# A one-core hybrid block kernel: three small moves in the order of the work at the start and the end of its mixer loop

## The chip, the cores and the metric

The kernel runs on one core of a Trainium2 chip. The metric is the device time of one execution in microseconds; of several executions the median is taken. TensorE (PE) multiplies matrices, VectorE (DVE), ScalarE (ACT) and GpSimd (POOL) do element-wise work, and SyncE (SP) issues the DMAs. Each engine runs its own instruction list in order, and the lists are tied together by semaphores: an instruction that waits holds up everything behind it on its engine.

## The reference

The reference computes a block with four parts, each added to a residual stream x of 2 x 512 tokens by 512 channels:

```python
x = x + masked_linear(layernorm(x))
x = x + ffn(layernorm(x))        # 4-bit weights, dequantized by group; silu(gate) * up, then down
x = x + mixer(layernorm(x))      # Mamba-2 style state space mixer
x = x + ffn(layernorm(x))        # the same weights
```

The mixer is most of the time. It projects the normalised tokens to a gate z, to x, B and C and to dt, runs a causal convolution of four taps with a silu over x, B and C, and works in chunks of 128 tokens:

```python
Y_diag = einsum('bclsh,bcshp->bclhp', (C @ B.T) * exp(segment_sum(A_dt)), x_dt)
Y_off  = einsum('bclhn,bchpn->bclhp', C, states) * state_decay
y = Y_diag + Y_off + D * x
y = y * rsqrt(mean(y ** 2) + eps) * norm_w
y = y * silu(gate)
out = y @ out_proj_w.T
```

There are 128 heads of 64 channels (8192 channels), 8 groups of B and C, and two batches of 512 tokens.

## The kernel before

**Precision.** Every large product is made of float32r operands split in two: a high part (a copy by ScalarE into float32r) and a low part (the value minus its high part). A product of two such operands is three matmuls per 128 rows of the contraction, `PASSES`: high by high, high by low, low by high. A projection of 512 channels has 4 x 3 = 12 matmuls of 128x512.

**Steps.** The mixer walks over 128 pairs of heads, k = 0 to 127 (K = 128), 64 to a batch, plus five steps to drain (`STEPS` = K + 1 + HALF = 133). A pair is 128 channels. In step k TensorE (`tensor`, in the class `Mixer`) does, in this order:

- `project(("x", k + 1))`: the projection of the next pair's x (L1016)
- `outputs(k - 1)`: y of the pair before (L1085, L1091)
- `turn_x(k)`: x turned to tokens by channels (L1056)
- `project(("z", k + 1))`: the gate of the next pair (L1016), and in some steps the projection of a group's B or C. `bc_units(k)` gives B of group 1 in step 3 and C of group 1 in step 4, and the later groups likewise, eight steps apart
- `project_out(i, t)`, one tile of the output projection (L1104)
- `states(k)`: the chunk states (L1069)

**Output projection.** Four pairs make a half group (`HALF` = 4), so there are 32 of them, i = 0 to 31. One half group's contribution to the four token tiles t = 0 to 3 of its batch is made one tile per step, four steps after its last pair. A tile is 4 pairs x 3 passes = 12 matmuls into one of three ring banks of PSUM; then VectorE adds it to the residual (`accumulate`, L1549). `project_out` waits until `yg_lo`, the count of low parts of y, and `wo_lo`, the count of low parts of output weights, have reached all four pairs. The last half group (i = 31, pairs 124 to 127) has its tiles in steps 129 to 132, when no pair is left to work on.

**VectorE** (`vector`) in step k: `y_low(k - 2)` (the low part of the gated y of two pairs before, L1538, which waits for `yg_hi`, ScalarE's high part), the accumulation of an output tile, `decay_c(k)` (L1511), `conv(("x", k + 1))` (three instructions, L1458, which wait for `tap_done`), `scale_x(k)` (x_dec and x_dt, L1479 and L1484) and `mask_em(k)` (L1519), `gate(k - 1)` (y and the gated y, which is written over sz, L1528 and L1532), `carry(k)` (the state carried over chunks, L1493 and L1499), and in steps 3 and 4 the convolution of B or C.

**ScalarE** (`scalar`) in step k: high parts of weights (`w_high`, L1243, and `wo_high`, L1311), `tap(("x", k + 1))` (the first tap of the convolution, out of the ring bank, L1255), `clamp(k + 1)` (eight small instructions, L1285), in an odd step `exponent(k + 1)` (L1295), `activate_x(k + 1)` (silu of x, L1260), `activate_z(k + 1)` (silu of the gate into `sz`, L1265), `y_high(k - 1)` (L1305) and `square(k - 1)` (L1299), which wait for the gated y, then in steps 3 and 4 the tap of B or C, and in an even step `exponent(k + 1)`. Exp and Silu need different function tables; the loads of these show as ACT_TABLE_LOAD.

**The buffer behind one wait.** `sz` has three slots. `activate_z` writes slot k % 3, so it has to wait until the low part of the pair three before has been read from it:

```python
def activate_z(k):
    act.wait_ge(prj_mm, UNIT["z", k] + 1)
    need(act, yg_lo, k - 2)
```

In step 2 it makes z of pair 3, which needs `yg_lo` at 1: `y_low(0)`, which VectorE does at the head of the same step.

**GpSimd** makes the low parts of the weights (L1688, L1693) and the running sum of y squared (L1705). **SyncE** loads the weights; a load waits until the slot's low part has been made, and of those slots there are two.

**After the last pair**, TensorE in step 128 turns two tiles of the second FFN's normalised input (L128), and in step 129 does the first tile of the last half group, `square_sums(1)` (eight products with a column of ones, L1118), and turns two more tiles. VectorE's `factor_mean(1)` (L1581) and `factor(1)` (L1587) and between them ScalarE's `factor_root(1)` (L1385, a square root with its own table) make the norm's factor out of these sums; `end_tile` (L1599) then finishes each token tile, and the second FFN (`ffn`, L410 and L422) begins. Its first products need all eight normalised tiles in high and low parts (`norm_low`, L140).

## Time and profile before

| | |
|---|---|
| median of 3 runs | 2114.71 us (2114.70 to 2115.32) |
| the profiled execution's own time | 2115.85 us |
| its span, from first to last instruction | 2114.1 us |
| TensorE busy | 2067.3 us, 98% of the span |
| VectorE, ScalarE, GpSimd busy | 78%, 67%, 42% |
| mean granted TensorE clock | 0.998 of 2.4 GHz |

The share of the clock is 1.00 for 2.4 GHz and 0.50 for 1.2 GHz. In a timeline row stand the start in us, the time in us, the engine, the line, the operation, what is written and read with its shape, the number of instructions merged in the row, and in brackets the idle time of the engine before it and who ended it. A row's time reaches to the end of its last instruction, while the next may have started. In the trace step 2 begins on TensorE at 333.80 us, step 5 at 372.32 us, and step 129 at 1862.62 us.

### The profile page before, as it was taken

How to read it: one execution, taken by the hardware profiler on the slowest of the kernel's cores; microseconds unless marked ns; L12 is line 12 of the kernel's file. 1: busy time of each engine (PE TensorE's matmuls, PEld its weight loads, DVE VectorE, ACT ScalarE, POOL GpSimd, SP SyncE). 2: the span in 40 equal slices, each digit the busy share in tenths (PEclk: the TensorE clock that was granted, in tenths of full speed). 3: DMA queues.
4: the chain of work that ended last, by engine and by line, in shares of the span. 5: the costliest groups of instructions: out<-in, count | busy, mean ns of one | idle time of the engine just before them, and what ended most of it. 6: DMA issues, size and time to landing. Idle time of an engine off the chain costs nothing.

```text
span 2114.1 us, 35693 instructions
## 1 busy us (share of the span) xinstructions
PE 2067.3 (98%) x12366; PEld 1703.4 (81%) x12366; DVE 1656.5 (78%) x2676; ACT 1424.1 (67%) x2690; POOL 887.6 (42%) x616
## 2 busy tenths in 40 slices
PE   7999998999999999999999999999999999989999
PEld 6788876788888888888888888888888888878887
DVE  7655557888888888888888888888888888876554
ACT  4322268878787878778787877877877878742221
POOL 1221214445454545454454544454545555422121
PEclk9999999999999999999999999999999999999999
DMA  5543225445444444444444444445444444455341
GB/s 204 176 139 136 78 85 184 151 140 158 147 138 154 139 154 148 150 160 133 142 156 150 144 155 134 150 154 162 139 155 140 154 149 145 148 172 172 131 147 40
DMA packets 160095, 307.06 MB, mean 145 GB/s; under 512 B 14528, under 2 KB 47552, under 8 KB 159680
## 3 DMA queue, kind: packets, MB, share of 16 engines
q1 hardware_dynamic: 159936, 305.00, 44.4%
q8 instruction: 92, 1.51, 0.3%
q14 instruction: 67, 0.55, 0.1%
HBM read 299.70 MB, written 5.24 MB: 144 GB/s over the span
## 4 chain that ended last, share of the span: by engine, by line
PE 78%; DVE 10%; issue 5%; ACT 4%; POOL 1%; DMA 1%; DVEq 0%; ACTq 0%; SPq 0%; POOLq 0%
PE ring L1016 30%; PE ring L1104 14%; PE bank L410 6%; PE bank_e L410 6%; PE yt L1085 5%; PE st L1069 4%; PE bank_e L422 3%; PE yt L1091 3%; PE bank L422 3%; PE xt L1056 3%; DVE xc L1458 1%; DVE ce L1511 1%; DVE em L1519 1%; DVE ygs L1538 1%; DVE bc L1458 1%
## 5 line engine op out<-in xcount | busy, mean ns | idle before, releaser
L1016 PE MATMUL ring<-m_lnt,w_sb 128*128 128x512 f32 x3456 | 858.9, 398 | 5.5 <-ACT sz L1265 2.5
L1016 PEld LDWEIGHTS ring<-m_lnt,w_sb 128*128 128x128 f32 x3456 | 630.1, 188 | 134.0 <-issue 3.1
L1688 POOL TENSOR_TENSOR w_sb<-w_raw,w_sb 128x512 fp32r<-128x512 f32 x288 | 428.4, 1490 | 162.3 <-ACT w_sb L1243 162.0
L1705 POOL TENSOR_TENSOR ysq<-ysq,y 128x512 f32<-128x512 f32 x126 | 169.8, 1348 | 637.2 <-ACT y L1299 637.2
L1104 PE MATMUL ring<-wo,ygs 128*128 128x512 f32 x1536 | 372.2, 392 | 5.6 <-DVE ygs L1538 3.3
L1104 PEld LDWEIGHTS ring<-wo,ygs 128*128 128x128 f32 x1536 | 289.2, 189 | 68.0 <-issue 7.8
L1458 DVE SCALAR_TENSOR_TENSOR xc<-ring,cw,xc 128x511 f32<-128x511 f32 (+2 forms) x384 | 286.8, 747 | 52.3 <-ACT xc L1255 43.2
L1285 ACT ACTIVATE cum_b<-cum_b,cum_q 128x128 f32<-128x128 f32 x1024 | 312.5, 390 | 0.0
L1243 ACT ACTIVATE w_sb<-w_raw 128x512 fp32r<-128x512 f32 x288 | 178.2, 620 | 48.0 <-DMA w_raw<-w_in 47.8
L1693 POOL TENSOR_TENSOR wo<-wo_raw,wo 128x512 fp32r<-128x512 f32 x128 | 191.1, 1493 | 1.6 <-ACT wo L1311 1.6
L1085 PE MATMUL yt<-em,x_dt 128*64 128x128 f32 x2048 | 183.9, 279 | 3.6 <-DVE state L1499 3.5
L326 POOL TENSOR_TENSOR f_gu<-f_gu_f,f_gu 128x1024 fp32r<-128x1024 f32 x28 | 67.3, 2404 | 257.7 <-ACT f_gu L349 257.7
L1511 DVE TENSOR_TENSOR ce<-ce,bc 128x768 f32<-128x768 f32 x128 | 171.6, 1340 | 1.9 <-DMA ce<-e_t 1.8
L1295 ACT ACTIVATE arg<-cum_b 128x1024 f32<-128x1024 f32 x128 | 131.8, 1029 | 60.8 <-DVE em L1519 59.6
L1305 ACT ACTIVATE ygs<-sz 128x512 fp32r<-128x512 f32 x128 | 80.2, 626 | 128.5 <-DVE sz L1532 126.4
L1085 PEld LDWEIGHTS yt<-em,x_dt 128*64 128x64 f32 x2048 | 118.5, 136 | 49.0 <-issue 49.0
L1519 DVE TENSOR_TENSOR em<-arg,gt 128x1024 f32<-128x1024 f32 x128 | 155.6, 1215 | 0.0
L410 PE MATMUL bank_e<-f_lnt,f_gu 128*128 128x512 f32 x672 | 154.3, 390 | 0.7 <-DVE f_lnt L140 0.7
L410 PE MATMUL bank<-f_lnt,f_gu 128*128 128x512 f32 x672 | 154.2, 390 | 0.6 <-DVE f_lnt L140 0.6
L1091 PE MATMUL yt<-ce,state 128*64 128x128 f32 x1536 | 149.7, 273 | 0.0
L410 PEld LDWEIGHTS bank_e<-f_lnt,f_gu 128*128 128x128 f32 x672 | 125.9, 188 | 27.1 <-DVE f_lnt L140 1.1
L410 PEld LDWEIGHTS bank<-f_lnt,f_gu 128*128 128x128 f32 x672 | 125.9, 188 | 27.1 <-DVE f_lnt L140 1.1
(198 smaller groups left out, 2891.9 us busy)
## 6 DMA issues: line engine op xcount, KB each, us to landing
w_raw<-w_in SPq DMA_DIRECT2D x288, 256.0 KB, 3.4
cum_b<-c_t SPq DMA_DIRECT2D x128, 512.0 KB, 4.6
ce<-e_t SPq DMA_DIRECT2D x128, 384.0 KB, 4.5
wo_raw<-w_out SPq DMA_DIRECT2D x128, 256.0 KB, 3.0
f_gu_q<-gu_w SPq DMA_DIRECT2D x28, 512.0 KB, 3.5
f_gu_zr<-gu_z SPq DMA_DIRECT2D x28, 512.0 KB, 4.3
f_gu_sr<-gu_s SPq DMA_DIRECT2D x28, 512.0 KB, 5.3
f_dn_q<-dn_w SPq DMA_DIRECT2D x28, 256.0 KB, 3.4
```

Of the source, the lines that this page charges most:

```text
L410: mm = nc.tensor.matmul(dst[half][:], gu[:, j, b, c:c + P], lnt[:, a, k, half * TOK:(half + 1) * TOK], start=(i == 0), stop=(i == 3 * KT - 1))
L1016: mm = nc.tensor.matmul(dst[:], w_sb[:, u % WR, wp, k * P:(k + 1) * P], lnt[:, xp, k, b * S:(b + 1) * S], start=(i == 0), stop=(i == 3 * K ...
L1085: mm = nc.tensor.matmul(YT[h * HD:(h + 1) * HD, c * CS:(c + 1) * CS], x_dt[:, at:at + HD], em[:, h, c * CS:(c + 1) * CS], start=True, stop ...
L1091: mm = nc.tensor.matmul(YT[h * HD:(h + 1) * HD, c * CS:(c + 1) * CS], state[:, c - 1, h * HD:(h + 1) * HD], ce[:, k % 2, h, (c - 1) * CS:c ...
L1104: mm = nc.tensor.matmul(dst[:], ygs[:, j % OR, yp, t * P:(t + 1) * P], wo[:, j % WOR, wp], start=(m == 0), stop=(m == 3 * HALF - 1))
L1243: nc.scalar.activation(w_sb[:, u % WR, 0], w_raw[:, u % NR], ACT.Copy).then_inc(w_hi, 1)
L1285: last = nc.scalar.activation(cum_b[:, k % 2, h, at], cum_b[:, k % 2, h, at], ACT.Relu, scale=-1.0, bias=cum_q[:, k, c, h:h + 1])
L1458: nc.vector.scalar_tensor_tensor(out=dst[:, d:S], in0=src[:, 0:S - d], scalar=cw[:, tile, j:j + 1], in1=dst[:, d:S], op0=ALU.mult, op1=ALU ...
L1511: nc.vector.tensor_tensor(ce[:, k % 2], ce[:, k % 2], c_off.rearrange("p (o t) -> p o t", o=1) .to_broadcast([P, 2, OFFC * CS]), ALU.mult) ...
L1519: nc.vector.tensor_tensor(em[:], ARG[:], gt[:, k // QG % 2].rearrange("p (o t) -> p o t", o=1).to_broadcast([P, 2, S]), ALU.mult).then_inc ...
L1688: nc.gpsimd.tensor_tensor(w_sb[:, u % WR, 1], w_raw[:, u % NR], w_sb[:, u % WR, 0].bitcast(F32), ALU.subtract).then_inc(w_lo, 1)
L1693: nc.gpsimd.tensor_tensor(wo[:, j % WOR, 1], wo_raw[:, j % 2], wo[:, j % WOR, 0].bitcast(F32), ALU.subtract).then_inc(wo_lo, 1)
```

## The change

There are three parts.

1. `project_out` for the first tile of the last half group (i = 31, t = 0) waits at first for one pair less in both counts, and waits for the fourth pair ahead of matmul 9, the first of its own three.
2. On VectorE `y_low(k - 2)` moves, for k = 2, 3 and 4, from the head of the step to behind `carry(k)`. From step 5 on it stays at the head.
3. On ScalarE the tap of B of group 1 (step 3) moves from behind `square(2)` to ahead of `activate_x(4)`. The other taps of B and C stay.

```diff
--- before.py
+++ after.py
@@ -1097,10 +1097,14 @@
                 def project_out(i, t):
                     dst = ring_bank(("out", (i, t)))
                     ring_free(("out", (i, t)))
-                    pe.wait_ge(yg_lo, HALF * (i + 1))
-                    pe.wait_ge(wo_lo, HALF * (i + 1))
+                    early = 1 if (i, t) == (K // HALF - 1, 0) else 0
+                    pe.wait_ge(yg_lo, HALF * (i + 1) - early)
+                    pe.wait_ge(wo_lo, HALF * (i + 1) - early)
                     for m, (j, (yp, wp)) in enumerate((j, ab) for j in range(HALF * i, HALF * (i + 1))
                                                       for ab in PASSES):
+                        if early and m == 3 * (HALF - 1):
+                            pe.wait_ge(yg_lo, K)
+                            pe.wait_ge(wo_lo, K)
                         mm = nc.tensor.matmul(dst[:], ygs[:, j % OR, yp, t * P:(t + 1) * P], wo[:, j % WOR, wp],
                                               start=(m == 0), stop=(m == 3 * HALF - 1))
                     mm.then_inc(out_mm, 1)
@@ -1411,6 +1415,8 @@
                     if k + 1 < K:
                         if k % 2:
                             exponent(k + 1)
+                        if k == 3:
+                            tap(("b", 1))
                         activate_x(k + 1)
                         activate_z(k + 1)
                     if 1 <= k <= K:
@@ -1419,7 +1425,8 @@
                     for unit in ahead[2:]:
                         w_high(unit)
                     for unit in bc_units(k):
-                        tap(unit)
+                        if k != 3:
+                            tap(unit)
                     for g in silu_in(k):
                         activate_bc(g)
                     if k + 1 < K and k % 2 == 0:
@@ -1623,7 +1630,7 @@
                             norm_shift(dve, n, i)
                     if k == K + 2:
                         factor_mean(1)
-                    if 2 <= k <= K + 1:
+                    if HALF < k <= K + 1:
                         y_low(k - 2)
                     if k == K + 1:
                         scale_gu(0, 0)
@@ -1667,6 +1674,8 @@
                         carry(k)
                     if k == 0:
                         conv(("x", 2))
+                    if 2 <= k <= HALF:
+                        y_low(k - 2)
                     if k == K - 1:
                         sub_gu(0, 0)
                     for g in gram_in(k):
```

**TensorE, end of step 128 and step 129.** bank_e5 is a turned tile of the FFN's input, ring1 the bank of the output tile, ysq the sum of squares. Before:

```order
L128 MATMUL bank_e5<-ident,f2_xn 128x128 [waits n2_xn_done,xdt_done]
L128 MATMUL bank_e5<-ident,f2_xn 128x128 x3
L1104 MATMUL ring1<-wo,ygs 128x512 [waits wo_lo,yg_lo,acc_done]
L1104 MATMUL ring1<-wo,ygs 128x512 x11
L1118 MATMUL arg<-ones,ysq 128x1 [waits em_done,ysq_done]
L1118 MATMUL arg<-ones,ysq 128x1 x3
L128 MATMUL bank_e6<-ident,f2_xn 128x128 [waits n2_xn_done,st_done]
```

Of the change:

```order
L128 MATMUL bank_e5<-ident,f2_xn 128x128 [waits n2_xn_done,xdt_done]
L128 MATMUL bank_e5<-ident,f2_xn 128x128 x3
L1108 MATMUL ring1<-wo,ygs 128x512 [waits wo_lo,yg_lo,acc_done]
L1108 MATMUL ring1<-wo,ygs 128x512 x8
L1108 MATMUL ring1<-wo,ygs 128x512 [waits wo_lo,yg_lo]
L1108 MATMUL ring1<-wo,ygs 128x512 x2
L1122 MATMUL arg<-ones,ysq 128x1 [waits em_done,ysq_done]
L1122 MATMUL arg<-ones,ysq 128x1 x3
L128 MATMUL bank_e6<-ident,f2_xn 128x128 [waits n2_xn_done,st_done]
```

The wait for the fourth pair stood ahead of all twelve matmuls and now stands ahead of the last three.

**VectorE, from the carry of step 1 to that of step 2.** ygs<-sz,ygs is `y_low`, ce is `decay_c`, state is `carry`. Before:

```order
L1493 COPY state<-st 128x128
L1499 SCALAR_TENSOR_TENSOR state<-state,e_last,st 128x64 x4
L1538 TENSOR_TENSOR ygs<-sz,ygs 128x512
L1511 TENSOR_TENSOR ce<-ce,bc 128x768
L1458 SCALAR_TENSOR_TENSOR xc<-ring2,cw,xc 128x511
L1458 SCALAR_TENSOR_TENSOR xc<-ring2,cw,xc 128x510
L1458 SCALAR_TENSOR_TENSOR xc<-ring2,cw,xc 128x509
L1479 TENSOR_TENSOR x_dec<-xt,dec_q 128x384
L1484 TENSOR_TENSOR x_dt<-xt,dt_q 128x512
L1519 TENSOR_TENSOR em<-arg,gt 128x1024
L1528 SCALAR_TENSOR_TENSOR y<-xc,d_col,yt 128x512
```

Of the change:

```order
L1518 TENSOR_TENSOR ce<-ce,bc 128x768
L1465 SCALAR_TENSOR_TENSOR xc<-ring2,cw,xc 128x511
L1465 SCALAR_TENSOR_TENSOR xc<-ring2,cw,xc 128x510
L1465 SCALAR_TENSOR_TENSOR xc<-ring2,cw,xc 128x509
L1486 TENSOR_TENSOR x_dec<-xt,dec_q 128x384
L1491 TENSOR_TENSOR x_dt<-xt,dt_q 128x512
L1526 TENSOR_TENSOR em<-arg,gt 128x1024
L1535 SCALAR_TENSOR_TENSOR y<-xc,d_col,yt 128x512
L1539 SCALAR_TENSOR_TENSOR sz<-y,nw,sz 128x512
L1500 COPY state<-st 128x128
L1506 SCALAR_TENSOR_TENSOR state<-state,e_last,st 128x64 x4
L1545 TENSOR_TENSOR ygs<-sz,ygs 128x512
```

The low part of pair 0 stood ahead of ce, and now stands behind the carry of step 2; what was behind that carry, the low part of pair 1, has gone behind the next.

**ScalarE, step 3 from the exponent on.** bc is B's tap, sz<-ring2 `activate_z(4)`, ygs<-sz `y_high(2)`. Before:

```order
L1295 ACTIVATE arg<-cum_b 128x1024 [waits em_done,arg_clamped]
L1260 ACT_TABLE_LOAD
L1260 ACTIVATE xc<-xc 128x512 [waits conv_done]
L1265 ACTIVATE sz<-ring2 128x512 [waits yg_lo,prj_mm]
L1305 ACTIVATE ygs<-sz 128x512 [waits yg_done]
L1299 ACTIVATE y<-y 128x512 [waits yg_done]
L1243 ACTIVATE w_sb<-w_raw 128x512 [waits prj_mm,w_loaded1]
L1255 ACTIVATE bc<-ring0,cb,cw 128x512 [waits prj_mm]
L1243 ACTIVATE w_sb<-w_raw 128x512 [waits prj_mm,w_loaded0]
L1311 ACTIVATE wo<-wo_raw 128x512 [waits wo_loaded0]
L1255 ACTIVATE xc<-ring1,cb,cw 128x512 [waits y_done,prj_mm]
```

Of the change:

```order
L1299 ACTIVATE arg<-cum_b 128x1024 [waits em_done,arg_clamped]
L1259 ACTIVATE bc<-ring0,cb,cw 128x512 [waits prj_mm]
L1264 ACT_TABLE_LOAD
L1264 ACTIVATE xc<-xc 128x512 [waits conv_done]
L1269 ACTIVATE sz<-ring2 128x512 [waits yg_lo,prj_mm]
L1309 ACTIVATE ygs<-sz 128x512 [waits yg_done]
L1303 ACTIVATE y<-y 128x512 [waits yg_done]
L1247 ACTIVATE w_sb<-w_raw 128x512 [waits prj_mm,w_loaded1]
L1247 ACTIVATE w_sb<-w_raw 128x512 [waits prj_mm,w_loaded0]
L1315 ACTIVATE wo<-wo_raw 128x512 [waits wo_loaded0]
L1259 ACTIVATE xc<-ring1,cb,cw 128x512 [waits y_done,prj_mm]
```

B's tap has moved ahead of the table load and the two silus; no table load is added.

## Rows read from the trace of the kernel before

**Rows 1.** The page: the span, and each engine's busy time.

```profile
span 2114.1 us, 35693 instructions
...
PE 2067.3 (98%) x12366; PEld 1703.4 (81%) x12366; DVE 1656.5 (78%) x2676; ACT 1424.1 (67%) x2690; POOL 887.6 (42%) x616
```

**Rows 2.** Waits of TensorE (who, for whom: us, times, longest).

```profile
PE st L1069 <- DVE x_dec L1479: 7.8, 8, 2.5
```

**Rows 3.** Windows view, steps 6 to 126: busy times, granted clock, DMA.

```profile
385.00:1845.00 1460.00, 1454.50 (x9466) 1201.03 (x9466) 1253.50 (x2058) 1170.28 (x2273) 731.95 (x510) 1.00 0.46 148
```

**Rows 4.** Timeline of TensorE, steps 2 to 5 (start, us, what, idle before).

```profile
344.27 0.94 PE L1069 MATMUL st<-x_dec,b_tok 128*128 128x128 f32 x6 [2.25 <-DVE x_dec L1479]
...
356.50 0.83 PE L1069 MATMUL st<-x_dec,b_tok 128*128 128x128 f32 x6
...
371.63 0.94 PE L1069 MATMUL st<-x_dec,b_tok 128*128 128x128 f32 x6 [2.47 <-DVE x_dec L1479]
...
382.94 2.97 PE L1104 MATMUL ring<-wo,ygs 128*128 128x512 f32 x12 [1.64 <-POOL wo L1693]
```

**Rows 5.** Timeline of ScalarE, the same steps.

```profile
344.67 0.59 ACT L1265 ACTIVATE sz<-ring 128x512 f32<-128x512 f32 x1
347.42 0.63 ACT L1305 ACTIVATE ygs<-sz 128x512 fp32r<-128x512 f32 x1 [2.17 <-DVE sz L1532]
...
362.94 0.77 ACT L1255 ACTIVATE bc<-ring,cb,cw 128x512 f32<-128x512 f32 x1
...
364.64 0.77 ACT L1255 ACTIVATE xc<-ring,cb,cw 128x512 f32<-128x512 f32 x1
...
374.78 0.63 ACT L1305 ACTIVATE ygs<-sz 128x512 fp32r<-128x512 f32 x1 [2.52 <-DVE sz L1532]
...
379.39 0.62 ACT L1311 ACTIVATE wo<-wo_raw 128x512 fp32r<-128x512 f32 x1
```

**Rows 6.** Timeline of VectorE, the same steps.

```profile
348.52 0.68 DVE L1538 TENSOR_TENSOR ygs<-sz,ygs 128x512 fp32r<-128x512 f32 x1
...
353.20 2.32 DVE L1458 SCALAR_TENSOR_TENSOR xc<-ring,cw,xc 128x511 f32<-128x511 f32 x3 [2.05 <-ACT xc L1255]
...
363.74 2.32 DVE L1458 SCALAR_TENSOR_TENSOR bc<-ring,cw,bc 128x511 f32<-128x511 f32 x3 [3.36 <-ACT bc L1255]
...
368.81 2.30 DVE L1458 SCALAR_TENSOR_TENSOR xc<-ring,cw,xc 128x511 f32<-128x511 f32 x3
```

**Rows 7.** Timeline of TensorE, steps 129 on and the FFN's start.

```profile
1862.62 5.46 PE L1104 MATMUL ring<-wo,ygs 128*128 128x512 f32 x12 [3.32 <-DVE ygs L1538]
...
1869.89 8.44 PE L1104 MATMUL ring<-wo,ygs 128*128 128x512 f32 x36
...
1886.29 16.62 PE L410 MATMUL bank_e<-f_lnt,f_gu 128*128 128x512 f32 x72 [0.69 <-DVE f_lnt L140]
```

**Rows 8.** Windows view, TensorE's first product of step 129.

```profile
1862.00:1868.00 6.00, 5.38 (x14) 4.25 (x14) 4.54 (x5) 4.49 (x7) 3.36 (x2) 0.50 0.74 262
```

**Rows 9.** Timeline of VectorE, steps 129 to 132.

```profile
1861.83 0.69 DVE L1538 TENSOR_TENSOR ygs<-sz,ygs 128x512 fp32r<-128x512 f32 x1 [0.69 <-ACT ygs L1305]
...
1865.27 1.27 DVE L140 TENSOR_TENSOR f_lnt<-bank_e,f_lnt 128x512 fp32r<-128x512 f32 x2
1869.24 0.16 DVE L1581 TENSOR_SCALAR eps_row<-arg 128x4 f32<-128x4 f32 x1 [2.70 <-PE arg L1118]
...
1869.92 0.17 DVE L1587 RECIPROCAL eps_row<-eps_row 128x4 f32<-128x4 f32 x1
...
1878.36 0.69 DVE L1549 TENSOR_TENSOR xr<-xr,ring 128x512 f32<-128x512 f32 x1 [0.33 <-PE ring L1104]
```

**Rows 10.** Timeline of ScalarE, steps 129 and 130.

```profile
1867.27 1.28 ACT L1385 ACT_TABLE_LOAD   x1
1869.43 0.21 ACT L1385 ACTIVATE eps_row<-eps_row 128x4 f32<-128x4 f32 x1 [0.89 <-DVE eps_row L1581]
```

## Prediction

> **What bounds the kernel now.** I read the page first. TensorE is busy for 2067.3 of 2114.1 us [rows 1], so all its idle time is 46.8 us, and a change of order can only win from that. Next came the windows view. From step 6 to step 126 TensorE is busy for 1454.5 of 1460 us at the full clock [rows 3]. A delay or a gain that reaches TensorE before 385 us is therefore kept to the end of the loop, since there is next to no idle time to swallow it. The view of waits puts 7.8 us on `states` waiting for x_dec [rows 2], and the timeline shows where: 2.25 us in step 2 and 2.47 us in step 4, then 1.64 us ahead of the first output tile [rows 4]. Last, the one long wait behind the loop: 3.32 us for the low part of y of pair 127, in step 129 [rows 7]. The change touches these two places, and I cost each by walking through it. A measurement of this kernel can tell a difference of about 0.2%, 4.2 us, from none; both terms below are smaller.
>
> **Low parts behind the carry: a new wait on ScalarE.** The move takes no work away. In step 2 VectorE gets to its convolution of x(3) sooner, but that waits for ScalarE's tap anyway, so `states(2)` stays at 344.27. What the move adds is behind `activate_z(3)`. It needs the low part of pair 0, and began at 344.67 [rows 5]. The low part of pair 0 now stands where that of pair 1 stood, right behind the carry of step 2: 348.52 to 349.20 [rows 6]. So ScalarE waits until 349.2, spends 0.5 us on z, and comes to `y_high(1)` at 349.7 in place of 347.42 [rows 5]. Of the 4.5 us wait, 2.17 us was idle time of ScalarE before; **2.3 us** is new delay. Queued behind it are the high part of B's weights, the exponent of step 3 and the tap of x(4).
>
> **Step 3.** The convolution of x(4) began at 353.20 after 2.05 us idle for that tap [rows 6], so it goes to 355.5. TensorE's `states(3)` began at 356.50 with no wait [rows 4]. From the step 4 pair of rows, `states` can begin 2.82 us behind the start of the convolution (368.81 to 371.63) [rows 4, 6]; so it could have begun at 356.0, and now begins at 358.3, 1.8 us later. The carry of step 3 and the low part of pair 1 behind it end at about 363.3, just as ScalarE comes to `activate_z(4)`, so there the slot costs nothing more.
>
> **B's tap ahead of the silus.** The tap was at 362.94 and the convolution of B at 363.74, after 3.36 us idle of VectorE [rows 5, 6]. The tap costs 0.77 us wherever it stands. In its new place it starts about when the exponent ends, at 361.3 with the delay. VectorE is free at 363.3, so the convolution of B ends at 365.5 and the decayed C (up to 2.0 us) at 367.5. The tap of x(5) ends at 364.64 + 0.77 + 2.3 = 367.7 [rows 5], and this now rules: the convolution of x(5) begins at 367.7 in place of 368.81 [rows 6], 1.1 us sooner. Moving the tap by itself would bring it to the tap's old end, 365.4, **3.4 us** sooner; the low parts take 2.3 of it back. TensorE's wait of 2.47 us in step 4 goes, but what is late next is ScalarE.
>
> **Step 4 and the first output tile.** `y_high(3)` was released by the gated y at 374.78, after 2.52 us idle [rows 5]. VectorE is 1.1 us sooner, but `activate_z(5)` ahead of it again waits for a low part behind the carry, the same pattern as in step 2, worth +2.3. So `y_high(3)` is at 374.78 - 1.1 + 2.3 = 376.0, 1.2 us late. Behind it stand the tap of C, the exponent and the high part of the output weights of pair 3 (379.39) [rows 5], which GpSimd's low part and the first output tile wait for. That tile began at 382.94 and was waiting for exactly this [rows 4]. **The first part costs 1.2 us.** Its bounds: 0.9 if B's weights go through GpSimd faster; 1.5 if VectorE's decayed C is slowed more.
>
> **The last half group.** The first three pairs are ready: pair 126's low part lands as the turns of step 128 end, at about 1859.1. Nine matmuls at full clock are 9 x 8.44 / 36 = 2.1 us [rows 7] and fill the wait to 1861.2. The low part of pair 127 ends at 1862.5 [rows 9]; the last three end at 1863.3. Before, the twelve took 5.46 us [rows 7] with the clock at 0.50, 1.2 GHz [rows 8], after the 3.32 us in which TensorE did nothing, and ended at 1868.1. So the product ends **4.8 us sooner**, 2.1 by the early start, the rest by the clock, if that stays up. But who waits for it? The sums of squares follow, and VectorE's mean stood at 1869.24 after 2.70 us idle [rows 9]. It can now run when `norm_low` ends, at 1865.27 + 1.27 = 1866.5 [rows 9]. ScalarE's root is behind its table load, which ends at 1867.27 + 1.28 = 1868.6 [rows 10], 0.9 us before the old 1869.43. VectorE's reciprocal stood at 1869.92 [rows 9], behind the accumulation of the first tile, which can now run ahead of it: it goes to 1868.6 + 0.2 = 1868.8, 1.1 us sooner. The rest of the end is VectorE's own chain, whose one wait for TensorE, 0.33 us at 1878.36 [rows 9], goes too. TensorE has its 36 matmuls [rows 7] done by 1876 and waits no less for VectorE at 1886.29 [rows 7]. **The end gains 1.1 + 0.33 = 1.4 us** out of 4.8.
>
> **The sum.** 2115.85 (the profiled execution, 1.75 above its span) + 1.2 - 1.4 = 2115.65. That execution was 1.14 above the median of the runs, 2114.71, so the forecast is **2114.5**: no change that can be told.
>
> **Where a rule of the skill speaks.** In this trace the clock was at 1.2 GHz after TensorE had stood idle, and TensorE worked its way back up [rows 7, 8]. The Trainium skill, "TensorE: Matmul & The Clock Gate", section "What's actually happening", says the low clock is the default and that activity releases it. By that rule a wait cut into pieces need not be enough; this is the second case.
>
> **The cases.**
> - *Forecast, 0.65.* Both walks hold: +1.2 and -1.4, 2114.5.
> - *The clock falls in the new gaps, 0.14.* The product ends sooner, so TensorE now stands idle behind it: from 1863.3 until the turn, whose input ScalarE makes at 1866.5, but for eight short products. If it falls there, some eight of the next 36 matmuls run at 5.46 / 12 = 0.455 us in place of 0.234 [rows 7], 1.8 us. They would end at 1877.8, and of the end's 1.4 us only 0.3 stays. Time: 2114.71 + 1.2 - 0.3 = 2115.6. For it: much idle, little work there. Against: with 2.25 and 2.47 us idle at a time in steps 2 and 4 [rows 4] the products behind ran at full pace.
> - *The new wait on ScalarE costs nothing, 0.12.* If the idle time that I count as used up is there after all, only B's tap counts: y_high(3) comes 3.4 sooner less about 1.0 for ScalarE's own queue, -2.4, and with the end -3.8: 2110.9. It speaks against it that the slot's wait is in the code.
> - *Slower, 0.09.* The one mechanism is the sz slot of step 2, with B's tap not making up for it. If VectorE, not the tap, bounds step 4 (B's convolution begins no sooner than 365.5, because it still waits for the tap), the convolution of x(5) is 2.3 late in place of 1.1 early. Then step 4's pattern adds 2.3 on top: +4.6, which is slower by over 0.2% if the end gains under 0.4, as when the clock falls. With the end's 1.4 it is 2117.9, with 0.3 it is 2119.0. The point from which it decides is that start of B's convolution, 365.5 against my 363.3.
>
> **Numbers.** The forecast with the clock's case spans 2113 to 2116.5. The range reaches down to near the third case and up towards the fourth: 2112.0 to 2117.2. Faster by over 0.2% needs the third case and more than its 3.8 us: 0.04. Slower by over 0.2% needs the fourth with little gained at the end: 0.05. Within 0.2%: 0.91.
>
> **What would show it.** Step by step: `activate_z(3)` with 4.5 us idle of ScalarE ended by VectorE's ygs, and `y_high(1)` 2.3 us late; `states(3)` about 1.8 us late, with a wait; `states(4)` without its 2.47 us; the first output tile about 1.2 us late. At the end nine matmuls, a gap of some 1.4 us and three at 2.4 GHz; the FFN's product of 1886.29 sooner by 1.4 us, counted from the turns of step 128. I am wrong if ScalarE does not wait in step 2, if the output tile is early, or if the clock is at 0.50 anywhere behind 1863.

## The result, and the profile after

| | before | after |
|---|---|---|
| median of the runs, us | 2114.93 (2112.54 to 2117.79, 16 runs) | 2118.98 (2117.28 to 2120.84, 16 runs) |
| profiled execution, us | 2115.85 | 2119.61 |
| its span, us | 2114.1 | 2117.9 |

The ratio is 1.0017, with a 95% interval of 1.0011 to 1.0024. The change makes the kernel about 4 us slower. That is 0.17 to 0.19%, just inside the 0.2% that the prediction called telling, but the interval excludes one. The prediction was 2114.5 with a range up to 2117.2, and the result is outside it. Of all the executions behind this document one, of experiment e8, took 2578.33 us at a mean granted clock of 0.754; it is left out of that run's ratio, and without it the median of e8 would be 2112.23 in place of 2112.29.

The page of the changed kernel, span and busy times:

```profile
span 2117.9 us, 35694 instructions
...
PE 2070.2 (98%) x12366; PEld 1705.2 (81%) x12366; DVE 1655.0 (78%) x2676; ACT 1424.8 (67%) x2690; POOL 888.2 (42%) x616
```

With the same 12366 matmuls TensorE is *busy* for 2.9 us more than in [rows 1]. An order that only made TensorE wait longer would add idle time. More busy time for the same matmuls points to the clock, so that is the first thing to look for.

To place the 4 us I cut both traces at the same instructions. **S** runs from the start of `states(2)` to the start of `states(5)`. **E** runs from the start of `states(127)` to the start of the FFN's product of 72 matmuls at L410. What lies between is the loop.

| us | before | after | difference |
|---|---|---|---|
| S | 41.47 | 45.54 | +4.07 |
| from there to `states(127)` | 1466.19 | 1466.29 | +0.10 |
| E | 34.36 | 34.13 | -0.23 |

The three add up to +3.94; the spans differ by 3.8, since `states(2)` itself starts 0.17 sooner after the change. S is 385.74 - 344.27 before and 389.64 - 344.10 after.

TensorE in the changed kernel, steps 2 to 5 (start, us, what, idle before and who ended it):

```profile
344.10 0.94 PE L1069 MATMUL st<-x_dec,b_tok 128*128 128x128 f32 x6 [2.25 <-DVE x_dec L1486]
...
358.24 0.94 PE L1069 MATMUL st<-x_dec,b_tok 128*128 128x128 f32 x6 [1.73 <-DVE x_dec L1486]
...
371.48 0.83 PE L1069 MATMUL st<-x_dec,b_tok 128*128 128x128 f32 x6
...
377.41 3.01 PE L1016 MATMUL ring<-m_lnt,w_sb 128*128 128x512 f32 x12
384.38 5.46 PE L1108 MATMUL ring<-wo,ygs 128*128 128x512 f32 x12 [3.96 <-POOL wo L1702]
389.64 1.21 PE L1069 MATMUL st<-x_dec,b_tok 128*128 128x128 f32 x6
```

Measured from `states(2)`, `states(3)` is 1.91 us late against [rows 4] (14.14 against 12.23), `states(4)` is as early as before and without its wait of 2.47 us, and the first output tile is 1.61 late (40.28 against 38.67). So far this is close to the walk. The row of the tile is not: in front of it TensorE is idle for 3.96 us where it was idle for 1.64, and the twelve matmuls take 5.46 us where they took 2.97 [rows 4].

ScalarE of the changed kernel, the same steps:

```profile
349.13 0.60 ACT L1269 ACTIVATE sz<-ring 128x512 f32<-128x512 f32 x1 [4.52 <-DVE ygs L1545]
349.63 0.62 ACT L1309 ACTIVATE ygs<-sz 128x512 fp32r<-128x512 f32 x1
...
371.29 0.63 ACT L1247 ACTIVATE w_sb<-w_raw 128x512 fp32r<-128x512 f32 x1 [3.85 <-DMA w_raw<-w_in]
...
375.75 0.60 ACT L1269 ACTIVATE sz<-ring 128x512 f32<-128x512 f32 x1 [0.96 <-DVE ygs L1545]
376.25 0.62 ACT L1309 ACTIVATE ygs<-sz 128x512 fp32r<-128x512 f32 x1
...
380.86 0.61 ACT L1315 ACTIVATE wo<-wo_raw 128x512 fp32r<-128x512 f32 x1
```

VectorE of the changed kernel, step 3:

```profile
363.10 2.31 DVE L1465 SCALAR_TENSOR_TENSOR bc<-ring,cw,bc 128x511 f32<-128x511 f32 x3
...
367.47 2.32 DVE L1465 SCALAR_TENSOR_TENSOR xc<-ring,cw,xc 128x511 f32<-128x511 f32 x3
```

The wait for the slot of sz is there, 4.52 us, and makes `y_high(1)` 2.4 late against [rows 5], again measured from `states(2)`. The convolution of B goes without its wait of 3.36 us [rows 6], and that of x(5) begins 1.2 sooner. In step 4 the pattern returns (0.96 us for the low part of pair 2), and the high part of the output weights of pair 3, at 380.86 in place of 379.39 [rows 5], is 1.6 late. So it is this that the first output tile waits for, by way of GpSimd.

One row here is in no step of the prediction: at 371.29 ScalarE has waited 3.85 us for a load of weights. Before, it stood here:

```profile
367.74 0.63 ACT L1243 ACTIVATE w_sb<-w_raw 128x512 fp32r<-128x512 f32 x1 [2.33 <-DMA w_raw<-w_in]
```

Measured from `states(2)` it is 3.7 us later. A load waits until GpSimd has made the low part of its slot, and GpSimd waits for ScalarE, so a delay of ScalarE in steps 2 and 3 comes back to it by way of the weights. Behind this row ScalarE stood idle for 0.43 and 2.52 us before, and for 0.96 us now; 3.7 less 2.95 plus 0.96 is 1.7 us, close to the measured 1.6 of `y_high(3)`.

The clock of TensorE, changed kernel, windows view (window; its length; busy us of TensorE, weight loads, VectorE, ScalarE and GpSimd; granted clock; DMA share; GB/s): the gap ahead of the first output tile, the tile, and three stretches of the end:

```profile
380.30:384.40 4.10, 0.14 (x2) 0.05 (x1) 3.74 (x6) 4.10 (x12) 3.37 (x3) 0.90 0.67 150
384.40:389.60 5.20, 5.20 (x12) 4.09 (x13) 3.69 (x6) 4.45 (x9) 1.08 (x1) 0.50 0.73 227
1868.00:1872.00 4.00, 2.31 (x14) 2.25 (x14) 3.21 (x6) 3.20 (x4) 2.08 (x1) 0.55 1.01 360
1872.00:1875.00 3.00, 3.00 (x10) 2.42 (x10) 2.07 (x4) 1.73 (x4) 0.28 (x1) 0.50 1.02 276
1875.00:1878.00 3.00, 3.00 (x14) 2.52 (x13) 2.02 (x4) 0.00 (x0) 0.00 (x0) 0.96 1.03 272
```

All of the first output tile ran at 0.50, that is at 1.2 GHz; the clock fell in the gap ahead of it, whose mean is 0.90. At the end it fell again, about 1868: the prediction's own sign of being wrong, a clock of 0.50 behind 1863, is in the row from 1872.

TensorE of the changed kernel, steps 129 on:

```profile
1863.18 2.33 PE L1108 MATMUL ring<-wo,ygs 128*128 128x512 f32 x9
1866.57 0.97 PE L1108 MATMUL ring<-wo,ygs 128*128 128x512 f32 x3 [1.06 <-DVE ygs L1545]
1867.72 1.27 PE L1122 MATMUL arg<-ones,ysq 128*128 128x1 f32 x8 [0.19 <-POOL ysq L1714]
1870.69 1.94 PE L128 MATMUL bank_e<-ident,f_xn 128*128 128x128 f32 x8 [1.70 <-ACT f_xn L120]
1872.28 9.80 PE L1108 MATMUL ring<-wo,ygs 128*128 128x512 f32 x36
...
1890.06 16.62 PE L410 MATMUL bank_e<-f_lnt,f_gu 128*128 128x512 f32 x72 [0.67 <-DVE f_lnt L140]
```

VectorE of the changed kernel, steps 130 to 132:

```profile
1870.47 0.15 DVE L1588 TENSOR_SCALAR eps_row<-arg 128x4 f32<-128x4 f32 x1
...
1872.80 0.18 DVE L1594 RECIPROCAL eps_row<-eps_row 128x4 f32<-128x4 f32 x1 [1.59 <-ACT eps_row L1389]
...
1876.68 0.69 DVE L1556 TENSOR_TENSOR xr<-xr,ring 128x512 f32<-128x512 f32 x1 [0.94 <-PE ring L1108]
...
1882.12 0.69 DVE L1556 TENSOR_TENSOR xr<-xr,ring 128x512 f32<-128x512 f32 x1 [0.33 <-PE ring L1108]
```

The product is split as planned, nine and three, at full pace. Then TensorE waits for ScalarE's f_xn, and the 36 matmuls take 9.80 us in place of 8.44 [rows 7]. VectorE waits for them twice, once for 0.94 us where it had no wait. Counted from `states(127)`, 4.00 us later in this trace, the reciprocal of the norm's factor stands at 1868.80, exactly where the walk put it, 1.1 us sooner than before. The wait of 0.94 us takes nearly all of that back.

### The profile page after: what moved, and what is told of

It reads as the page before. It is cut to its first block, busy times and chain, and to the rows that moved or that the text cites. A ratio compares the mean times of both kernels' runs of the same rounds, so it can differ in the third digit from the quotient of the medians.

```text
span 2117.9 us, 35694 instructions
## 1 busy us (share of the span) xinstructions
PE 2070.2 (98%) x12366; PEld 1705.2 (81%) x12366; DVE 1655.0 (78%) x2676; ACT 1424.8 (67%) x2690; POOL 888.2 (42%) x616
## 4 chain that ended last, share of the span: by engine, by line
PE 80%; DVE 10%; issue 5%; ACT 4%; POOL 1%; DMA 0%; DVEq 0%; ACTq 0%; SPq 0%; POOLq 0%
PE ring L1016 30%; PE ring L1108 14%; PE bank L410 6%; PE bank_e L410 6%; PE yt L1085 5%; PE st L1069 4%; PE bank_e L422 3%; PE yt L1091 3%; PE xt L1056 3%; PE bank L422 3%; DVE xc L1465 1%; DVE em L1526 1%; DVE ce L1518 1%; DVE ygs L1545 1%; DVE bc L1465 1%
## 5 line engine op out<-in xcount | busy, mean ns | idle before, releaser
L410 PE MATMUL bank_e<-f_lnt,f_gu 128*128 128x512 f32 x672 | 154.4, 390 | 0.7 <-DVE f_lnt L140 0.7
L410 PE MATMUL bank<-f_lnt,f_gu 128*128 128x512 f32 x672 | 154.1, 390 | 0.6 <-DVE f_lnt L140 0.6
L410 PEld LDWEIGHTS bank_e<-f_lnt,f_gu 128*128 128x128 f32 x672 | 125.9, 188 | 27.2 <-DVE f_lnt L140 1.1
L410 PEld LDWEIGHTS bank<-f_lnt,f_gu 128*128 128x128 f32 x672 | 125.9, 188 | 27.1 <-DVE f_lnt L140 1.1
```

The lines of the kernel that those rows point to most:

```text
L410: mm = nc.tensor.matmul(dst[half][:], gu[:, j, b, c:c + P], lnt[:, a, k, half * TOK:(half + 1) * TOK], start=(i == 0), stop=(i == 3 * KT - 1))
```

## The experiments

The theory at this point: of the 4.07 us in S, about 1.6 is the order (the wait for the slot less what B's tap gives), carried through to the first output tile, and about 2.4 (5.46 - 2.97 = 2.49) is the clock. At the end the clock takes back what the early start gives. The rival: the order alone costs the whole, and the clock only shows where TensorE would wait anyhow, so that keeping it up changes nothing.

All twelve in one table. "Tile" is the idle time ahead of the first output tile and its length; "last" is the product of step 129 and the 36 matmuls behind. S, E and these lengths are of one profiled execution each. Each median stands beside runs of before on the same chip (medians 2114.77, 2115.26 and 2115.4 for the three groups that ran together, 32 to 35 runs each).

| run | median us | ratio, 95% | S | tile | E | last |
|---|---|---|---|---|---|---|
| before | - | - | 41.47 | 1.64 / 2.97 | 34.36 | 5.46, 8.44 |
| the change | 2118.98 | 1.0017, 1.0011 to 1.0024 | 45.54 | 3.96 / 5.46 | 34.13 | 2.33 + 0.97, 9.80 |
| e1 end alone | 2117.0 | 1.0003, 0.9994 to 1.0012 | 41.42 | 1.62 / 3.00 | 34.27 | 2.32 + 0.97, 9.94 |
| e2 first steps alone | 2118.72 | 1.0014, 1.0005 to 1.0023 | 45.48 | 3.97 / 5.46 | 33.15 | 4.57, 8.46 |
| e3 low parts alone | 2120.39 | 1.0026, 1.0016 to 1.0035 | 46.28 | 3.96 / 4.58 | 33.14 | 4.39, 8.44 |
| e4 tap alone | 2114.58 | 0.9997, 0.9988 to 1.0006 | 42.15 | 2.88 / 5.46 | 32.55 | 3.00, 8.42 |
| e5 change, gap filled | 2116.57 | 1.0010, 1.0001 to 1.0018 | 43.12 | 0.47 / 3.01 | 33.64 | 2.32 + 0.98, 9.47 |
| e6 change, fourth slot | 2114.93 | 0.9999, 0.9990 to 1.0008 | 39.82 | 2.88 / 3.01 | 34.59 | 2.33 + 0.96, 10.27 |
| e7 tap, gap filled | 2112.92 | 0.9992, 0.9983 to 1.0001 | 39.81 | 0.21 / 2.97 | 33.19 | 4.38, 8.47 |
| e8 tap, end split, both filled | 2112.29 | 0.9985, 0.9977 to 0.9994 | 39.75 | 0.23 / 2.99 | 32.57 | 2.32 + 0.96, 8.43 |
| e9 before, end filled | 2114.25 | 0.9996, 0.9987 to 1.0005 | 41.32 | 1.62 / 3.00 | 32.55 | 3.00, 8.43 |
| e10 change, first tile split | 2117.69 | 1.0009, 1.0000 to 1.0018 | 41.96 | 1.59 / 0.93 for the last three | 34.48 | 2.31 + 0.96, 10.14 |
| e11 tap, both split, end filled | 2112.35 | 0.9984, 0.9975 to 0.9993 | 38.68 | 0.90 / 0.94 for the last three | 32.55 | 2.31 + 0.96, 8.45 |
| e12 as e11, with the low parts and a fourth slot | 2112.0 | 0.9983, 0.9974 to 0.9992 | 38.58 | 0.88 / 0.93 for the last three | 32.54 | 2.31 + 0.96, 8.43 |

The loop between S and E took 1465.7 to 1467.7 in all of these, without a pattern that I could see. S and E leave that scatter out and so tell more than the medians, but each is one execution.

**The parts apart: e1 to e4.** e1 has only the split of the last product; e2 only the first steps:

```
-                    early = 1 if (i, t) == (K // HALF - 1, 0) else 0
+                    early = 0
```

e3 has, of the first steps, only the low parts behind the carry, and e4 only B's tap; both with `early = 0`. In e3 B's tap goes back:

```
-                        if k == 3:
-                            tap(("b", 1))
...
-                        if k != 3:
-                            tap(unit)
+                        tap(unit)
```

and in e4 the low parts:

```
-                    if HALF < k <= K + 1:
+                    if 2 <= k <= K + 1:
                         y_low(k - 2)
...
-                    if 2 <= k <= HALF:
-                        y_low(k - 2)
```

Expected of e1:

> Only the split wait of the last half group's first tile; both moves of the first steps undone. Theory (the clock falls once more behind the product, as in the trace of the change, 0.60 in 1868 to 1870 us): 0.2 to 0.3 us faster than before, the FFN's first long product sooner by the same, the 36 matmuls behind in 9.8 us. Rival (that fall came of where the first steps had left the rest of the program; alone the split keeps the clock up): 1.4 us faster, the 36 matmuls in 8.4 us.

Of e2:

> Both moves of the first steps, without the split wait. Theory (the sz slot costs 1.6 us up to the first output tile, and the 3.96 us that TensorE then stands idle bring it to 1.2 GHz for that tile, 5.46 us in place of 2.97): 4.1 us slower than before, first output tile at 5.4 to 5.5 us. Rival (the loss comes from the two ends together): 1.5 to 2 us slower.

Of e3:

> Only the low parts behind the carry. Theory: without B's tap the sz slot's pattern adds up, the high part of y of pair 3 is 4.5 us late in place of 1.6, TensorE waits over 3 us for the output tile's weights and does it at 1.2 GHz: 4.5 + 2.5, so 7 us slower than before. Rival without the clock: 4.5 us slower. Rival in which ScalarE's wait is harmless and B's tap does the harm: within 1 us of before.

Of e4:

> Only B's tap ahead of the silus. Theory: convolution of x(5) 3.4 us sooner, high part of y of pair 3 and the first output tile 2.4 us sooner, TensorE idle ahead of it for about 2.6 us with the clock up: 2.4 us faster than before. If the clock falls there after all: 0.1 us slower. Rival in which the tap does the harm: 1 us slower or more.

The parts add up: e2's S is that of the whole change (45.48 and 45.54), and e1's is that of before (41.42 and 41.47). e2's median is 3.95 us above that of before, as expected (4.1). In e1 the 36 matmuls took 9.94 us, as the theory had it, and its rival (8.4) is out. Its median was to be 0.2 to 0.3 below that of before and is 2.2 above, with an interval on both sides of one. In its trace, 1.6 us longer than that of before, the excess is in the loop (1467.37) and ahead of `states(2)` (344.84), not in S or E.

e3 was expected to lose 7 us and lost 5.6 (2120.39 against 2114.77), 4.8 of it in S. The tile began after the same idle time, 3.96 us, but took 4.58 us. The windows view of e3, the gap and then the tile in three pieces, shows why:

```profile
382.30:386.30 4.00, 0.04 (x2) 0.04 (x1) 3.64 (x6) 4.00 (x12) 3.36 (x3) 1.00 0.68 160
386.30:387.30 1.00, 1.00 (x4) 0.87 (x5) 1.00 (x2) 0.61 (x3) 1.00 (x1) 0.89 0.69 212
387.30:388.30 1.00, 1.00 (x3) 0.71 (x3) 1.00 (x3) 0.68 (x1) 0.09 (x1) 0.50 0.83 265
```

The clock stayed up through the whole gap and fell when TensorE was already at work again. Without that (4.58 - 2.97 = 1.61) the low parts alone cost 46.28 - 41.47 - 1.61 = **3.2 us** in S. Both terms of the expectation were too large, 4.5 and 2.5.

e4 was expected to gain 2.4 with the clock up, or to lose 0.1 if it fell. It fell, and the median is 0.2 below that of before, nothing that can be told (S +0.7): TensorE comes to the tile sooner, waits 2.88 us there in place of 1.64, and the tile is at 1.2 GHz. The windows view of e4, gap and tile:

```profile
377.90:380.80 2.90, 0.03 (x1) 0.02 (x1) 2.54 (x4) 2.90 (x10) 2.90 (x3) 0.85 1.09 217
380.80:386.00 5.20, 5.19 (x12) 4.11 (x13) 3.72 (x6) 4.45 (x8) 1.11 (x1) 0.50 0.81 244
```

Without the clock (2.49) its S is 39.66, 1.8 us sooner than before. The order pays and the clock takes it.

That the order pays 1.8 and not 2.4 is seen on ScalarE of e4:

```profile
368.81 0.63 ACT L1247 ACTIVATE w_sb<-w_raw 128x512 fp32r<-128x512 f32 x1 [3.76 <-DMA w_raw<-w_in]
...
372.69 0.62 ACT L1309 ACTIVATE ygs<-sz 128x512 fp32r<-128x512 f32 x1
```

The convolution of x(5) is 3.4 us sooner here, as predicted, but it is not what `y_high(3)` waits for any more: from the load of weights on ScalarE has no idle time. That load came 1.4 us later than before (counted from `states(2)`), so `y_high(3)` is only 1.7 sooner. Why the load is later no run separates; GpSimd, whose low parts release it, starts its sum of y squared 0.65 us later, behind ScalarE's square, which now stands behind B's tap.

**The gap filled: e5 and e7.** Ahead of the wait for the first output tile, 14 (e5, on the change) or 12 (e7, on e4) matmuls on tiles that lie ready go to the same bank. The tile's own first matmul starts the bank anew, so nothing of this reaches the output; it is work added, none left out.

```
+                    if (i, t) == (0, 0):
+                        for _ in range(14):
+                            nc.tensor.matmul(dst[:], w_sb[:, UNIT["z", 6] % WR, 0, 0:P], lnt[:, 0, 0, 0:S],
+                                             start=True, stop=True)
```

> The changed kernel with 14 idle matmuls of 128x512 (3.2 us) on TensorE between the gate's projection and the first output tile of step 5, written to that tile's bank and overwritten by it. Theory (the 3.96 us idle before the tile bring the clock down, and that costs 2.5 us): the tile takes 2.9 to 3.0 us again and starts where it did, 384.4; 2.5 us faster than the change, 1.1 to 1.6 slower than before. Rival (the tile is slow for its own sake, its operands arriving late): no gain, a tile of 5.46 us.

> B's tap alone with 12 idle matmuls ahead of the first output tile. Theory: the tile at 380.8 as in the run with the tap alone, but 2.9 to 3.0 us long in place of 5.46: 2.4 to 2.6 us faster than before and than the tap alone. Rival (the matmuls delay the tile or the clock falls later): no gain.

TensorE of e5:

```profile
380.19 3.49 PE L1103 MATMUL ring<-m_lnt,w_sb 128*128 128x512 f32 x14
384.16 3.01 PE L1112 MATMUL ring<-wo,ygs 128*128 128x512 f32 x12 [0.47 <-POOL wo L1706]
387.00 0.83 PE L1069 MATMUL st<-x_dec,b_tok 128*128 128x128 f32 x6
```

Its windows view, gap and tile:

```profile
380.10:384.10 4.00, 3.53 (x15) 2.55 (x14) 3.64 (x6) 4.00 (x12) 3.34 (x3) 1.00 0.78 166
384.10:387.10 3.00, 2.94 (x13) 2.46 (x14) 2.97 (x5) 2.27 (x5) 1.16 (x1) 1.00 0.70 208
```

The tile starts as late as in the change (40.28 us behind `states(2)` in both), the clock is at 1.00 throughout, and S still falls from 45.54 to 43.12: **2.42 us for the clock alone**. The rival, that the order costs the whole, is out. The medians go the same way: 2.4 below the change and 1.3 above before, as expected. And this does not rest on one trace each: the record has the mean granted clock of every execution, to a thousandth. It is 0.996 or 0.997 in all 16 of the change (mean 0.9967) and 0.997 to 0.999 in the 11 of e5 (mean 0.9983); 5.2 us at half the clock in 2118 us make 0.0012.

What is left, 43.12 - 41.47 = **1.65 us, is the order**: the wait for the slot, less what B's tap gives. e7 gives the tap without the clock: 39.81, so B's tap ahead of the silus is worth **1.66 us**, not the 2.4 predicted. With e3's 3.2 the two make +1.5, which agrees with e5's 1.65. e7's median is 2.3 lower (2112.92 against 2115.26), near the expected 2.4 to 2.6, though the interval just includes one. That agreement is partly luck: S gave only 1.66, and in the trace another 1.17 is at the end (E 33.19), where e7 changed nothing.

**A fourth slot: e6.** Until step 60 the silu of every fourth z goes into a row buffer (`x_row`) that has no other use yet, so ScalarE needs the low part of the pair three before, not two:

```
+        def sz_slot(k):
+            if k >= 60:
+                return sz[:, k % 3]
+            return x_row[:] if k % 4 == 3 else sz[:, k % 4]
...
-                    need(act, yg_lo, k - 2)
+                    need(act, yg_lo, k - 3 if k < 60 else k - 2)
```

> The changed kernel with a fourth slot for the gated y in the first steps (a row buffer that is free until step 68), so that the gate's silu of step k + 1 no longer needs the low part of step k. Theory (the slot is what ScalarE waits for): the 4.5 us idle in step 2 gone, states of step 3 without its 1.7 us wait, the first output tile some 3.5 to 4 us sooner than in the change and about where B's tap alone puts it, 380.8. In total 2 to 4 us faster than the change, as far as the clock lets it. Rival (the low parts' new place delays by itself): less than 1 us.

ScalarE of e6, step 2:

```profile
344.93 0.58 ACT L1274 ACTIVATE x_row<-ring 128x512 f32<-128x512 f32 x1
347.68 0.63 ACT L1314 ACTIVATE ygs<-sz 128x512 fp32r<-128x512 f32 x1 [2.17 <-DVE sz L1544]
```

The wait of 4.52 us is gone and ScalarE's 2.17 us of idle time ahead of `y_high(1)` is back, as in [rows 5]. S is 39.82, within 0.01 of that of e7 and 3.3 below that of e5, which has the clock up too but three slots. So the slot is the whole price of the low parts (3.3 here, 3.2 by e3), and also: once it costs nothing, **the low parts' new place gains nothing**: ScalarE then waits 3.79 us for the same load of weights as in e4. The tile is 3.3 us sooner than in the change (3.5 to 4 were expected) and the median 4.05 lower (expected 2 to 4). The tile here began after 2.88 us idle, as in e4, and yet ran at full pace. The windows view of e6, gap and tile:

```profile
378.60:381.50 2.90, 0.02 (x2) 0.03 (x1) 2.54 (x4) 2.90 (x9) 2.90 (x3) 1.00 1.02 220
381.50:384.30 2.80, 2.80 (x12) 2.32 (x13) 2.80 (x5) 2.07 (x5) 1.11 (x1) 1.00 0.70 225
```

**The end: e8 and e9.** e8 is e4's order with the end's split, e7's twelve matmuls, and two fills at the end: four matmuls ahead of the wait for pair 127, six behind the sums of squares. They go to the bank of the next tile, which starts it anew.

```
+                            warm(4)
                             pe.wait_ge(yg_lo, K)
...
                         square_sums(1)
+                        warm(6)
```

> B's tap and the split wait, low parts left at the head of the step; idle matmuls in the gaps: 12 ahead of the first output tile, 4 in the split and 6 behind the sums of squares. Theory: 2.5 us at the start and 1.4 us at the end with the clock at 2.4 GHz throughout: 3.5 to 4 us faster than before. Rival (the end gains nothing, TensorE is not waited for): 2.5 us faster.

e9 is the kernel before with twelve such matmuls ahead of the wait, and nothing else.

> The kernel before with 12 idle matmuls (2.7 us) ahead of the last half group's first tile, no split. Theory (the end gains only what the clock costs, the early start of nine matmuls nothing): from the last states to the FFN's long product 32.6 us in place of 34.4, as with split and filling together; 1 to 1.8 us faster than before (its own runs have the slow product only in part: 5.46, 4.57, 4.38 and 3.0 us were seen). Rival (the early start is what gains): 34.3 us as before less 0.3.

TensorE of e9, step 129 on:

```profile
1859.40 3.02 PE L1101 MATMUL ring<-wo,ygs 128*128 128x512 f32 x12 [0.44 <-DVE xr L1558]
1862.29 3.00 PE L1113 MATMUL ring<-wo,ygs 128*128 128x512 f32 x12
1867.46 8.43 PE L1113 MATMUL ring<-wo,ygs 128*128 128x512 f32 x36
```

e8 brought E to 32.57 and the median to 2112.29, 3.0 below that of before where 3.5 to 4 were expected (S gave 1.7 of the 2.5, E 1.8 in place of 1.4). e9, without any split, has E = 32.55. And e4, where the clock stayed up through 3.33 us of idle time with nothing done about it, has 32.55 too. So **all of the 1.8 us of the end is the clock, and the split itself is worth nothing**. VectorE of e4 shows why:

```profile
1866.91 0.14 DVE L1588 TENSOR_SCALAR eps_row<-arg 128x4 f32<-128x4 f32 x1
...
1869.25 0.18 DVE L1594 RECIPROCAL eps_row<-eps_row 128x4 f32<-128x4 f32 x1 [1.59 <-ACT eps_row L1389]
```

Without the split, but at full clock, the sums are there when VectorE comes to its mean, and its next wait is 1.59 us for ScalarE's root, the same as in the change. Counted from `states(127)` the mean starts at 14.56 us in e4 and at 14.54 in the change.

e9's median was 1.15 below that of before, in the expected 1 to 1.8, though the interval of its ratio includes one. (The 4.57, 4.38 and 3.0 us that its expectation names are from e2, e7 and e4, which have the order of before at the end.)

Put side by side, the traces say one thing more. In the five with the split and no fill at the end (the change, e1, e5, e6, e10) the clock fell ahead of the 36 matmuls, and E is 33.64 to 34.59. In the five with neither (before, e2, e3, e4, e7) the 36 took 8.42 to 8.47 us and E is 32.55 to 34.36, with before's own trace the slowest. The -0.23 in E is therefore a comparison with the worst of the ends that the old order gave. Each of the five with the split is longer than each of the other four, by 0.4 us at the least, though all are single traces.

**The first tile split: e10 to e12.** e10 gives the first output tile the same split:

```
-                    early = 1 if (i, t) == (K // HALF - 1, 0) else 0
+                    early = 1 if (i, t) in ((0, 0), (K // HALF - 1, 0)) else 0
...
-                            pe.wait_ge(yg_lo, K)
-                            pe.wait_ge(wo_lo, K)
+                            pe.wait_ge(yg_lo, HALF * (i + 1))
+                            pe.wait_ge(wo_lo, HALF * (i + 1))
```

> The changed kernel with the same split at the first tile of all (step 5): nine matmuls before the wait for pair 3's weights. Theory: they fill 2.0 of the 3.96 us idle, the clock stays up, and the tile ends 4.5 us sooner (2.5 for the clock, 2.0 for the start); the states behind it then wait for VectorE's x_dec, so 3.5 to 4 us of it count: within 1 us of before. Rival (the tile's end is not waited for, as at the end of the loop): 2.5 us faster than the change.

TensorE of e10:

```profile
380.50 2.34 PE L1108 MATMUL ring<-wo,ygs 128*128 128x512 f32 x9
384.43 0.93 PE L1108 MATMUL ring<-wo,ygs 128*128 128x512 f32 x3 [1.59 <-POOL wo L1702]
386.17 0.94 PE L1069 MATMUL st<-x_dec,b_tok 128*128 128x128 f32 x6 [0.81 <-DVE x_dec L1486]
```

Real work in the gap does what the added work did, and more: S is 41.96, 3.6 less than the change. What is late next is x_dec, 0.81 us. The median, 2117.69, shows only a part of that: it is 1.3 below the change and 2.3 above before, where within 1 us was expected. In the trace the clock fell in another place: a product of step 1 took 4.57 us behind 2.06 us of idle time.

```profile
325.72 4.57 PE L1016 MATMUL ring<-m_lnt,w_sb 128*128 128x512 f32 x12 [2.06 <-POOL w_sb L1697]
```

That execution was still the fastest of the eleven (2116.13), so this one product does not explain the median. The mean granted clock of the eleven is 0.9975 against 0.9983 in e5, which fits clock lost elsewhere; where, is not shown.

e11 is e4's order with both splits and the end's fills; e12 is e11 with the low parts behind the carry and the fourth slot.

> B's tap, the split at the first and at the last half group's first tile, idle matmuls at the end alone (4 and 6), low parts at the head of the step. Theory: the start 3.4 us shorter than before (tap 2.4, and 1.0 until x_dec), the end 1.8: 4.5 to 5.2 us faster than before. Rival (VectorE keeps the start at the tap's gain): 4 us faster.

> The same with the low parts behind the carry and the fourth slot that takes ScalarE's wait away. Theory: once the slot is not waited for, the low parts' place is worth 0 to 1 us in the start beyond the run without them. Rival (their place matters, since VectorE's head of the step is shorter): 2 us more.

TensorE of e11:

```profile
377.17 2.20 PE L1117 MATMUL ring<-wo,ygs 128*128 128x512 f32 x9
380.27 0.94 PE L1117 MATMUL ring<-wo,ygs 128*128 128x512 f32 x3 [0.90 <-POOL wo L1710]
```

e12 was expected within 0 to 1 us of e11, and is. Both are as fast as e8 and the fastest here, about 3 us (0.16%) below the kernel before and, by the medians, 7 below the change. e11 was expected to gain 4.5 to 5.2 and gained 3.0 in the medians; S and E did gain 2.8 and 1.8. The profiled executions do differ by 5.1; the medians differ by less, in part because the kernel before does not lose its 1.8 us at the end every time (e9's median gained 1.15). The rest isn't accounted for: the loop in between differs by up to 2 us from run to run. S of e12 is within 0.1 of e11's: the second time that the low parts' place shows no effect.

## Why the prediction was wrong

- **"Low parts behind the carry: a new wait on ScalarE."** Right: 4.52 us against 4.5, `y_high(1)` 2.4 late against 2.3. The slot costs 3.2 us by itself (e3), and e6 shows it to be the only effect of the edit that reaches TensorE.
- **"Step 3."** Right: `states(3)` 1.9 late against 1.8.
- **"B's tap ahead of the silus."** The walk held (convolution of B at 363.10 against 363.3, of x(5) at 367.47 against 367.7). Its worth alone was put at 2.4 when e4 was planned (and in the third case) and is 1.66 (e7): of the 3.4 us that VectorE gains, 1.0 was taken off for ScalarE's own queue, but the queue is held up by a load of weights that came 1.4 later, and takes 1.7.
- **"Step 4 and the first output tile."** This step failed. The start of the tile was put 1.2 late, as 1.1 sooner for VectorE and 2.3 for the slot; it is 1.61 late in the trace, and in e5 the order costs 1.65. So the number was near, but the path was not the one written down: `y_high(3)` no longer followed VectorE's convolution, it followed a load of weights that came 3.7 late and then 0.96 for the slot. What matters more is what was left out, the length of the tile itself, which the sum put at no change. I counted that TensorE's wait of 2.47 us in step 4 goes and that the tile starts later, each for its own sake. Put together they say that TensorE comes to the tile no later (0.7 us sooner in the trace) and waits there until it is ready, 1.6 later: 1.64 + 0.7 + 1.6 = 3.96 us, as near as the rounding goes. The clock fell in it, and twelve matmuls took 5.46 us. e5 prices that at 2.42 us, more than half of the whole loss. The term "the first part costs 1.2 us" is 4.07 us in the trace.
- **"The last half group."** Forecast -1.4, measured -0.23. This step failed too. The walk held up to the reciprocal, 1.1 sooner; the step "the 36 matmuls done by 1876" did not, for it took them at full clock, and the 0.33 of wait that was to go is still there. The product was split and ran at full pace as said, but the case "the clock falls in the new gaps", with its 0.3, is what happened: 9.80 us for the 36 matmuls, and VectorE waits 0.94 us for them. That case had 0.14. What spoke against it was that 2.25 and 2.47 us idle in steps 2 and 4 did no harm. e6's 2.88 us did no harm either, and e4's 2.88 did; a gap that once left the clock up is no evidence that it always will. Beyond that, the walk credited 2.1 of the product's 4.8 us to the early start. e9 and e4 show that none of the end's gain needs it: at full clock the old order gives 1.8 us, more than the 1.4 forecast. And the forecast was counted from one trace of before, in which the whole product was slow.
- **The sum.** +1.65 for the order, +2.42 for the clock in S, -0.23 in E, +0.1 in the loop: 3.9 us, against 3.8 between the spans. In its mechanism the case of the clock came nearest, but I let it act at the end alone, where my walk had just made the larger gap in the first steps. By the number the case "slower" fits, with its 2119.0, but that is luck: it rested on B's tap not making up, and its sign, a convolution of B no sooner than 365.5, did not appear (363.10). B's tap did its part.

The Trainium skill, "TensorE: Matmul & The Clock Gate", section "What's actually happening", has the low clock as the default and activity as what releases it. The traces agree as far as they go: the clock is at 0.50 behind the gaps of the change and of e4, and where the gap was filled to 0.21 to 0.90 us (e5, e7, e8, e11, e12) the matmuls behind it kept their full pace. But 2.88 us idle in e6 and 3.33 in e4 left it up. I cited it and gave it a place, and did not carry it to every gap that the walk made longer.

## What to carry to other kernels

When an order is walked through, write down for the fullest engine not only when each piece starts but how long it is idle ahead of it. Where a TensorE gap grows by 2 us, price the product behind it at both clocks. Here that more than doubled a loss (1.65 and 2.42 us) and once took all of a gain (e4). Gaps can be filled with real work that is ready (nine of a tile's twelve matmuls) or with matmuls that nobody reads, and the second is a cheap experiment that tells the clock's share from the order's. Before an instruction that frees a buffer is moved back, look for who waits for that buffer on another engine. And when an engine's wait is removed, look for its next one: here it was a load of weights, which capped the gain of B's tap. Last, an end counted from one trace is worth no more than that trace: the same order gave 32.55 to 34.36 us.

## What was unexpected of the hardware

The length of a gap does not settle what the clock does. 2.88 us idle was followed by a product of 5.46 us in e4 and of 3.01 in e6. 3.33 us at the end was followed by 3.00 in e4, by 5.46 before, and by 4.38 to 4.57 in e2, e3 and e7. 3.96 us was followed by 5.46 in the change and 4.58 in e3, where the clock was still up when work began again. Even 2.06 us was followed by 4.57 in e10, where e11 had 3.00 behind 2.13 us in the same place. So in these traces a gap of 2.06 to 3.33 us cost anything from nothing to 2.5 us for twelve matmuls, and one of 3.96 cost something each of the three times. What decides it stays open; nothing here shows it to be chance. Nor is it shown that the runs of one kernel spread for that reason. In the 100 executions of before that stand beside the experiments, the 22 with a mean clock of 0.997 took 2115.6 us on average and the 17 with 0.999 or 1.000 took 2114.7: about 1 us of a spread of 6.3, as far as a figure rounded to a thousandth can tell. The loop's 2 us from run to run stay open too.
